# A graph attention layer's edge stage: gather depth, ring, softmax order and weight loading changed together

## What is computed

```python
src, dst = (edge_index[0], edge_index[1])
enc = x
for l in range(L):
    q = (x @ Wq[l] + bq[l]).reshape(N, H, D)
    k = (x @ Wk[l] + bk[l]).reshape(N, H, D)
    v = (x @ Wv[l] + bv[l]).reshape(N, H, D)
    a = (q[dst] * k[src]).sum(-1) * scale
    amax = jax.ops.segment_max(a, dst, num_segments=N)
    e = jnp.exp(a - amax[dst])
    denom = jax.ops.segment_sum(e, dst, num_segments=N)
    alpha = e / (denom[dst] + 1e-16)
    agg = jax.ops.segment_sum(alpha[:, :, None] * v[src], dst, num_segments=N).reshape(N, C)
    x = agg + (x @ Ws[l] + bs[l]) + enc
```

## Time and profile before

| | us |
|---|---|
| median of 3 runs (3384.03 to 3386.51) | 3386.14 |
| the profiled execution | 3403.18 |
| its span, first to last instruction | 3401.4 |
| PE, PEld busy in it | 2660.2, 1887.6 |
| DVE, ACT, POOL busy in it | 2266.3, 829.6, 1642.9 |

### The profile page before, as it was taken

How to read it: one execution, slowest core, us unless ns; L and a number is a source line. 1 busy time by engine, 2 the same in 40 slices (tenths; PEclk the granted TensorE clock), 3 DMA queues, 4 the chain that set the end, 5 groups by cost and what they waited for, 6 DMA issues and landing times. The chain is left out here.

```text
span 3401.4 us, 43825 instructions
## 1 busy us (share of the span) xinstructions
PE 2660.2 (78%) x9872; PEld 1887.6 (55%) x9872; DVE 2266.3 (67%) x3504; ACT 829.6 (24%) x1638; POOL 1642.9 (48%) x1559
## 2 busy tenths in 40 slices
PE   2999787664877778997876658777776799969998
PEld 1788343333655556873443336555555577647776
DVE  5666688888766655446898887666547345476655
ACT  0454222221000011002222210000145323155544
POOL 0110667665566651106676656666514235344444
PEclk8999567776999998995667769999988899979999
DMA  1654666664566665436666646666642422261111
GB/s 58 211 197 171 196 195 198 193 191 124 161 194 198 198 184 180 139 115 200 193 199 194 193 116 173 192 194 193 183 168 99 136 99 99 85 198 38 37 37 36
DMA packets 215838, 524.38 MB, mean 154 GB/s; under 512 B 30652, under 2 KB 48424, under 8 KB 215238
## 3 DMA queue, kind: packets, MB, share of 16 engines
q0 software_dynamic: 100160, 328.28, 34.0%
q1 hardware_dynamic: 98182, 161.91, 14.2%
q10 hardware_dynamic: 17280, 31.63, 2.5%
HBM read 439.83 MB, written 81.88 MB: 153 GB/s over the span
## 5 line engine op out<-in xcount | busy, mean ns | idle before, releaser
L1488 PE MATMUL edge_psA<-layer_q_space 128*128 128x256 f32 (+1 forms) x2656 | 670.2, 400 | 200.0 <-DVE layer_q_space L1374 185.8
L1251 POOL DMA_INDIRECT edge_ring<-v_rows,edges_src x626 | 615.1, 983 | 370.6 <-DMA edge_ring<-v_rows,edges_src 197.3
L1251 POOL DMA_INDIRECT edge_ring<-k_rows,edges_src x626 | 591.5, 945 | 322.4 <-DMA edge_ring<-k_rows,edges_src 173.7
L1443 PE MATMUL edge_psQ<-layer_q_space,edge_hotT 128*128 x1328 | 575.3, 582 | 170.0 <-DVE layer_y_space L1296 132.6
L1488 PEld LDWEIGHTS edge_psA<-layer_q_space 128*128 128x128 f32 x2656 | 489.3, 193 | 380.7 <-issue 318.2
L1374 DVE TENSOR_TENSOR layer_q_space<-edge_ring,edge_psQ 128x512 f32<-128x512 f32 x664 | 434.6, 683 | 171.2 <-SPq L1219 168.0
L1443 PEld LDWEIGHTS edge_psQ<-layer_q_space,edge_hotT 128*128 128x128 f32 x1328 | 337.9, 279 | 373.2 <-issue 317.9
L1296 DVE TENSOR_TENSOR layer_y_space<-edge_psQ,edge_ring 128x512 f32<-128x512 f32 x664 | 423.7, 682 | 138.1 <-issue 52.1
L106 PE MATMUL proj_psP<-proj_w,proj_xT 128*128 128x512 f32 x1920 | 470.8, 403 | 12.6 <-DVE proj_w L886 5.5
L106 PEld LDWEIGHTS proj_psP<-proj_w,proj_xT 128*128 128x128 f32 x1920 | 361.8, 191 | 99.5 <-DVE proj_w L886 6.9
L1280 DVE TENSOR_REDUCE layer_scores<-layer_y_space 128x32 f32<-128x2048 f32 x166 | 377.6, 2275 | 0.1
(11 more groups left out here) (290 smaller groups left out, 2835.7 us busy)
## 6 DMA issues: line engine op xcount, KB each, us to landing
agg_rows<-layer_q_space ACTq DMA_DIRECT2D x40, 260.0 KB, 3.7
base_rows<-proj_enc SPq DMA_DIRECT2D x40, 256.0 KB, 2.0
k_rows<-proj_out ACTq DMA_DIRECT2D x40, 256.0 KB, 2.9
v_rows<-proj_out ACTq DMA_DIRECT2D x40, 256.0 KB, 2.5
edge_ring<-k_rows,edges_src POOLq DMA_INDIRECT x626, 3.7
edge_ring<-v_rows,edges_src POOLq DMA_INDIRECT x626, 3.7
ffn_downT<-down_rows SPq DMA_DIRECT2D x11, 512.0 KB, 10.2
proj_agg<-agg_rows SPq DMA_DIRECT2D x20, 260.0 KB, 3.0
```

The costliest lines, as they stand in the source:

```text
L1251: pool.indirect_dma_start(ring[:, (n + 1) % NB, :], None, rows, bass.IndirectOffsetOnAxis(ap=T["src"][:, t:t + 1], axis=0)).then_inc(lande ...
L1443: last = pe.matmul(psQ[i][:], hotT[j % 2][:, i * P:(i + 1) * P], one(qp[:, k, bass.ds(tiles[i], 1), :]), start=(k == 1), stop=(k == 0))
L1488: last = pe.matmul(psA[:, bass.ds(d % 2, 1), e, 0:hi - lo].rearrange("p o w -> p (o w)"), hot[:, s % R, :], wv[:, s % R, lo:hi], start=Fal ...
```

## The change

- **FLIGHT 4**: POOL waits for gather n - 4 instead of n - 3.
- **NV = 40** places in `ring`. The k rows use the first 32; the other eight hold `prod`, which leaves `y_space` (11 x 512 to 3 x 512 columns). The v rows use all 40: v gathers 32 to 39 wait until all scores are reduced (`reduced`), from 40 on for `weighted` at t - 19. The places of a k gather are shifted (K_FIRST), and a table `landing` holds semaphore and count of each gather.
- **Buffers**: `psQ` has QB = 6 buffers, two of them halves of `psA`'s first part; `R` is 16; `wv` now begins where the softmax's four rows lay.
- **Softmax's end**: the two whole-width operations are cut into the six parts and interleaved with the subtractions; ACT instead of DVE copies the weights out, each part behind the next part's exponential. PE waits for `hots` and `beside` once in four slots.
- **Projection weights**: all sixteen blocks go to the half of q's space in which the low parts of q are written later (`w_rows`). In layer 0 they are issued in `index_edges`, behind the edge loads; in layer 1 in `combine_project`, each with a semaphore of its own and no wait between. `raw` remains in layer 0 for the FFN weights. `index_edges` keeps its masks and a small table in the same space, and `diff` is laid over `spread`.

```diff
@@ constants
+NV = 40
+K_FIRST = NB - ET % NB
+V_FIRST = NV
@@ index_edges, SP
+                for i in range(4 * KC):
+                    j, k = divmod(i, KC)
+                    sp.dma_start(T["w_rows"][:, i, :], a[f"L0_gnn_W{names[j]}"][0, k * P:(k + 1) * P, :]
+                                 ).then_inc(w_in, 16)
                 sp.wait_ge(kept_rows, len(blocks))
...
+                sp.wait_ge(w_in, 16 * 4 * KC)
@@ normalise_project and combine_project
-                        if i >= RAW:
-                            sp.wait_ge(w_lows, i + 1 - RAW)
-                        sp.dma_start(raw[:, i % RAW, :], a[f"L0_gnn_W{n}"][layer, k * P:(k + 1) * P, :]
-                                     ).then_inc(w_in[i % RAW], 16)
+                        sp.dma_start(T["w_rows"][:, i, :], a[f"L0_gnn_W{n}"][layer, k * P:(k + 1) * P, :]
+                                     ).then_inc(w_in[i], 16)
@@ edge_attention
-        B, R = 4, 8
+        B, R, QB = 4, 16, 6
-        ring = m.sb("ring", [P, NB, C])
+        ring = m.sb("ring", [P, NV, C])
-        prod = y_space[:, 0:2 * B * C].rearrange("p (i c) -> p i c", c=C)
+        prod = ring[:, NB:NB + 2 * B, :]
-        psQ = [m.ps(f"psQ{i}", [P, C]) for i in range(B)]
+        psQ = [m.ps(f"psQ{i}", [P, C]) for i in range(B)] + [psA[:, 0, i, :] for i in range(QB - B)]
+        buffer = [(n + K_FIRST) % NB for n in range(ET)] + [t % NV for t in range(ET)]
+        landing = [(landed[u], 16 * buffer[:n + 1].count(u)) for n, u in enumerate(buffer)]
@@ edge_attention, POOL
-                FLIGHT = 3
+                FLIGHT = 4
...
-                        old = n - FLIGHT
-                        pool.wait_ge(landed[(old + 1) % NB],
-                                     old // NB * 16 + 16 if (old + 1) % NB else (old + 1) // NB * 16)
+                        pool.wait_ge(*landing[n - FLIGHT])
...
+                    elif t < NV:
+                        pool.wait_ge(reduced, BATCHES)
                     else:
-                        pool.wait_ge(weighted, t - NB + NT + 1)
+                        pool.wait_ge(weighted, t - NV + NT + 1)
@@ edge_attention, DVE
-                for n, (g, k) in enumerate(parts):
-                    s = slice(g * P, (g + k) * P)
-                    vec.tensor_tensor(rows[:, s], rows[:, s], top[:, s], ALU.subtract).then_inc(ready, 1)
-                for n, (g, k) in enumerate(parts):
-                    vec.wait_ge(returned, n + 1)
-                    vec.tensor_copy(by_g[:, g:g + k], pst[n % 2][:, 0:k, :].rearrange("p k (c h) -> p k c h", c=CH)
-                                    ).then_inc(stored, 1)
+                for n in range(len(parts) + 2):
+                    if n < len(parts):
+                        vec.scalar_tensor_tensor(out=top[:, at[n]], in0=first[:, at[n]], scalar=shared[:, 0:1],
+                                                 in1=top[:, at[n]], op0=ALU.add, op1=ALU.max).then_inc(lifted, 1)
+                    if 1 <= n <= len(parts):
+                        vec.wait_ge(lifted, n)
...
@@ edge_attention, PE
-                        if j:
-                            pe.wait_ge(multiplied, j * B + i - B + 1)
+                        if j * B + i >= QB:
+                            pe.wait_ge(multiplied, j * B + i - QB + 1)
```

More of the change, by code:

```diff
@@ L44 @@
 NB = 32
-V_FIRST = ET % NB + 1
+NV = 40
+K_FIRST = NB - ET % NB
+V_FIRST = NV
 AW = C + H
@@ L374, in index_edges @@
         seg = m.sb("seg", [P, RUN])
-        diff = m.sb("diff", [P, RUN])
-        masks = m.sb("masks", [P, MASKS], BF16)
+        diff = spread
+        masks = T["q_space"][:, 0:MASKS // 2].bitcast(BF16)
+        w_in = m.sem("w_in")
         masked, masks_out = m.sem("masked"), m.sem("masks_out")
@@ L615, in normalise_project @@
         psP = [m.ps(f"psP{i}", [P, C]) for i in range(4)]
-        w_in = [m.sem(f"w_in{i}") for i in range(RAW)]
         bias_in = m.sem("bias_in")
@@ L969, in combine_project @@
         psP = [m.ps(f"psP{i}", [P, C]) for i in range(4)]
-        w_in = [m.sem(f"w_in{i}") for i in range(RAW)]
+        w_in = [m.sem(f"w_in{i}") for i in range(4 * KC)]
         bias_in = m.sem("bias_in")
```

108 lines of the change are left out of this document (54 added, 54 removed).

## The result

The changed kernel took 3216.3 us (median of 4 runs, 3214.5 to 3217.22), the kernel before 3385.09 on the same chip (4 runs, 3381.23 to 3386.51): a ratio of 0.950, 95% interval 0.949 to 0.952, 169 us less. The forecast was 3231 in a range of 3185 to 3305. The profiled execution of the changed kernel took 3214.5 us with a span of 3212.4. Against the span of before that is 189 us, not 169: the execution profiled before was 17 us above its kernel's median, this one is not. Two slow runs, one of the kernel before at 6236.5 us beside e5 to e8 and one of e8 at 9623.8 us, are left out of all figures.

The account below looks back on a forecast made before the run. POOL's row of gathers, waiting on landings, was taken to pace both long stages. Terms of -72.5 us per layer, twice, and -10 for projections gave 3248 profiled, 3231 us as median; range 3185 to 3305.

Parts of the forecast that it names:

- -23 in k: k stage: with four gathers under way, 403 us instead of 426 from first to last gather, -23 us per layer.
- the pace of v: Rest of the v gathers: shorter distances between gathers give 36 of the 47.3 us saved per layer.
- The v ring: v stage: with 40 places, eight gathers fewer remain behind the full ring, 11.5 us per layer.
- the projections: Start of each layer: earlier weight loads save 7.5 us in layer 0 and 2.5 in layer 1, together -10.
- The late landings: Both gather stages: allowance over POOL's 1.25 us pace, 3.3 plus 9 us in k and 16 in v's rest.
- The softmax: Between k and v: interleaved parts and copies by ACT save 3.2 us per layer, bounds 0 and -5.
- The tail of k: From last k gather to last score: not shortened, since slots keep step with gathers; +1 us per layer.
- (a): Gather landings: memory or queues cannot serve faster, so landings stretch to 5.5 us; about 3325 us, chance 0.10.
- (c): Gather queue, both stages: landings stretch so far that the kernel is slower; 3524 us at 6.2 us each, chance 0.03.
- (b): k stage: the DVE with PE becomes the bound, so only v gains; 3277 us, chance 0.16.
- (e): POOL: the limit of four never acts because POOL waits elsewhere (ring, SP's signals); 3347 us, chance 0.03.
- (d): Both gather stages: no late landings remain and slots at k's end run closer behind gathers; 3191 us, chance 0.10.

Follow-up runs that it names:

- e5: The changed kernel unaltered, run again as the reference for the other runs: 3226.9 us, 0.947 of the kernel before.
- e8: The kernel before with only the change's loading of the projection weights: 3398.4 us, 0.997 of the kernel before.
- e1: The changed kernel with three gathers under way instead of four (FLIGHT 3): 3359.4 us, 0.985 of the kernel before.
- e3: The kernel before with four gathers under way instead of three and nothing else: 3262.7 us, 0.958 of the kernel before.
- e2: The changed kernel with six gathers under way instead of four (FLIGHT 6): 3184.7 us, 0.935 of the kernel before.
- e4: The changed kernel with POOL treating the v ring as 32 places instead of 40: 3243.4 us, 0.953 of the kernel before.
- e12: e11 with four psQ buffers instead of six: 3159.6 us, 0.929 of the kernel before.
- e10: The changed kernel with the softmax's end as before (whole-width operations, copies by the DVE): 3219.5 us, 0.946 of the kernel before.
- e9: The changed kernel with eight wv and one-hot buffers instead of sixteen (R = 8): 3226.5 us, 0.949 of the kernel before.
- e7: The changed kernel with two more semaphore increments by POOL before gathers (k from gather 32, every v): 3227.3 us, 0.948 of the kernel before.
- e11: The changed kernel with six gathers under way and the spread rows loaded by ACT instead of SP: 3158.9 us, 0.928 of the kernel before.

## Why the prediction was right, and where its terms were off

**The mechanism held at each step.** The pace of both long stages was POOL's gathers waiting for the third landing back (e1, e3), and what replaced it is POOL's own 1.25 us (e2, 1.250 us on average in v and none over 1.27). Depth alone gave -144 us in e3. The prediction's own terms for it, -23 in k and -36 for the pace of v, make -118; the -146 expected of e3 was worked out from the profile after. The v ring is worth its eight distances (e4), the projections -10 us in both pairs of profiles. psQ is worth nothing (e12), as it was costed, but the sentence that the deeper psQ is what makes the DVE fit is wrong: with four buffers and PE's clock at 0.73 k took 398.4 us (e3).

**The late landings were over-charged.** In k I left 3.3 us for the masks and 9 for the rest over the floor of 390: 12.3. The changed profile has 7.3 and 5.6, the mask wait of 4.2 included. For the rest of v I left 16 over 341.3; it has 8.3 and 7.3 (the floor was one distance too long: 272 of them are 340.0, and over that it has 9.6 and 8.5). This term, "9 us that I leave" and "16 us", was set by feel and not from a row. The trace allowed better: before, 96 of the 312 distances in k of layer 0 were over 1.35 us, and the parts above 1.25 add up to 36.0 us; one distance more of slack covers all of them but the few with over 1.55 of idle. 10 and 6 such distances are left in k, 17 and 17 in v. Layer 1 besides had more to lose than layer 0, for which alone I had made the sum: 428.6 and 406.5 us before, not 425.8 and 404.6.

**The softmax was under-charged.** I took 0.6 us for each of the fifteen 512-column instructions. The scalar ones start 0.66 us apart: 789.46, 790.79 and 791.45 in the timeline above, with two in the first row. So the subtractions end 26.5 us after the first scan began instead of 25.4, and of the 2.15 us that ACT's copies gain, 1.1 is lost. -1.0 and -1.2 per layer stood where -3.2 was forecast. The gain of the copies was itself over-charged: I had them end 1.3 us behind the last subtraction, and they end 2.57 behind it (802.48), since ACT then still has an exponential of 512 columns and one of 128 to do between them, with two waits of 0.2 us for PE; before it was 4.72. The cost of the cutting lies in the operation and not in POOL: a whole-width operation takes 3.02 us for 2688 columns, 0.575 for each 512 of them, with POOL's gathers beside both of them (e10) as where the last gather ends 0.8 us into the second (before), and the next part starts after 0.66. Here the rule of the Trainium skill that I weighed ("SBUF — State Buffer", SBUF: two separate sides) agrees with the trace on one side: POOL's gathers are stretched to 1.62 us beside the short operations and to 3.46 beside a long one. The other side, a DVE operation held for a whole gather, appears in none of these rows, and the row was the better guide for the sum.

**R was costed at nothing and gives 2 us per layer.** With eight places the DVE, working alone off a full ring, waits for PE's release of wv (0.72, 0.34, 0.21 and 0.34 us in layer 1 of the kernel before, the first of them in the row below); with sixteen it does not, and the first gather behind the full ring comes after 17.1 us instead of 19.1 (e9 gives it back). I had looked for its cover in the stretches where POOL is the bound. This is the one stretch of v in which the DVE is.

```profile
2035.97 0.69 DVE L1364 TENSOR_TENSOR layer_q_space<-edge_psQ,edges_local 128x512 f32<-128x512 f32 x1 [0.72 <-PE edge_psA L1488]
```

**The ring filled, as forecast**: gather 39 was through 62.5 us after the last k gather (62 said), with a POOL wait of 21.2 us behind it (15 to 25 said). The tail of k did not grow by the 1 us forecast: in layer 0, 310 slots were begun at the last k gather before and after.

**From the profiled execution to the median I was wrong.** The profile of before lay 17 us over its median and I took the same 17 off the result; the changed kernel's profile lies at its median. The gain by medians is 169 us against the 155 forecast; by the profiled spans it is 189. So by the profiles the terms are short by 34 us, nearly all in the two long stages. The forecast time is therefore nearer to the measured one than its terms are. The new kernel's profile does not lie 17 us above its median, so taking 17 us off was an error, and it made up for half of the 34: that is luck. Nearly all of the 20 us between the two comparisons come from the execution in which before was profiled; e8 at 3398 us has the same v stage and a longer k stage (404.6 and 431.5 in layer 0, against 404.6 and 425.8). In which stages the kernel before is faster where it takes 3385 us was not seen, since none of those executions has a profile.

**The rivals.** (a) and (c), stretched landings, fall: 3.7 us in the median with three, four and six under way. The Trainium skill ("DMA: Bandwidth & Descriptors", Latency and other measured facts) gives 2 us for an access at high load; no such increase shows in the landings of any run here, at up to 224 GB/s. (b) falls: the DVE was 90% busy, and k took 398 even with four psQ buffers. (e) falls with e1. (d) is what happened in part, late landings fewer than charged; its other half, slots closer behind the gathers, needed SP's order undone.

## What to carry to other kernels

When a producer waits for its own transfers, compare latency / (number under way) with the time that the producer itself needs for one: here 3.7 / 3 was just under 1.25, which left every third distance late (over 1.35 us). More depth than equality cost nothing here, since the ring was there, and took the scatter away as well (in v four gave 1.28 to 1.29 us, six 1.250). Then look for what ties other engines to the order of arrivals: a load issued in program order behind waits that it does not need was worth 15 us per layer, and it was in the trace before as a wait of PE.

## What the runs showed that I had not expected

- Two more semaphore instructions on POOL before each of about 1200 gathers cost nothing: 1.25 us stays 1.25 (e7), and so does the idle 0.30 between two gathers.
- With six gathers of 256 KB allowed under way they land as fast as with three, 3.7 us in the median, at a DMA share of 0.74 to 0.77.
- PE's granted clock in the k stage of layer 0 rose from 0.68 of full to 0.77 with the faster gathers, and its busy time fell from 307.4 us to 266.4 for the same matmuls. The stage does not follow it: k takes 391.6 us at 0.77 in e2 and 392.4 at 0.73 in e11. Why the clock differs stays open.
- The kernel before took 3385 us in one group of runs and 3403 to 3407 in the others; the changed kernel differed less, 3216 and 3227. Why stays open.
- Open: gather 40 of v still waits for 21 weighted slots, 6.3 and 7.5 us of idle in the two layers of e11. A release that follows the true last slot of an edge tile was not tried.
